# Causal attention rewritten: float32r stacks of 48 rows, two heads on the halves of the array, loads on GpSimd's queue

## The reference

```python
def _L0_attn_ref(x, Wq, Wk, Wv):          # x = layernorm of (8, 1024, 256), 16 heads of 16
    q = jnp.einsum('bte,hed->bhtd', x, Wq)
    k = jnp.einsum('bte,hed->bhtd', x, Wk)
    v = jnp.einsum('bte,hed->bhtd', x, Wv)
    scores = jnp.einsum('bhtd,bhsd->bhts', q, k)
    causal = jnp.tril(jnp.ones((T, T), dtype=bool))
    scores = jnp.where(causal, scores, -jnp.inf)
    scores = scores / jnp.sqrt(jnp.asarray(E, dtype=scores.dtype))
    w = jax.nn.softmax(scores, axis=-1)
    out = jnp.einsum('bhts,bhsd->bhtd', w, v)
    return jnp.transpose(out, (0, 2, 1, 3)).reshape(B, T, -1)
```

## Time and profile before

| | |
|---|---|
| median of three runs | 5360.85 us (5360.44 to 5373.26) |
| the profiled execution | 5367.81 us, span 5366.0 us |
| busy in the span | PE 4533.1, DVE 3604.8, ACT 2700.2, POOL 1211.8 us |
| mean granted clock of the array | 0.929 |
| attention | the first 1641 us or so |

### The profile page before, as it was taken

The page is one execution under the profiler, slowest core; times in us unless marked ns, Lnnn a source line. Parts: engine busy times, 40 slices in busy tenths (PEclk is TensorE's granted clock), DMA queues, the critical chain, the costliest instruction groups (busy, mean ns, idle before and its releaser), DMA issues. The chain is left out here.

```text
span 5366.0 us, 74844 instructions
## 1 busy us (share of the span) xinstructions
PE 4533.1 (84%) x23444; PEld 2361.1 (44%) x23444; DVE 3604.8 (67%) x6564; ACT 2700.2 (50%) x3784; POOL 1211.8 (23%) x784
## 2 busy tenths in 40 slices
PE   4888888887885888888888888888878999999999
PEld 1444344443432455445544554555553444444443
DVE  6677676676754878887888788555555555655653
ACT  0444444444453443444344434222226888888888
POOL 1000000000001333333333333000003455455454
PEclk7899899998997899989989999999998999999999
DMA  5422423324221000000000000000016666666664
GB/s 116 58 52 41 70 38 54 56 38 73 38 26 46 1 0 0 0 0 0 0 0 0 0 0 0 12 1 0 0 16 153 158 147 155 153 146 158 153 144 112
DMA packets 158004, 297.05 MB, mean 55 GB/s; under 512 B 41488, under 2 KB 88976, under 8 KB 141200
## 3 DMA queue, kind: packets, MB, share of 16 engines
q1 hardware_dynamic: 149760, 285.18, 25.9%
q10 hardware_dynamic: 7920, 7.87, 0.5%
HBM read 237.67 MB, written 55.31 MB: 55 GB/s over the span
## 5 line engine op out<-in xcount | busy, mean ns | idle before, releaser
L1686 ACT ACTIVATE gelu_out<-hidden,b_col 128x1024 f32<-128x1024 f32 x1024 | 1085.7, 1112 | 170.3 <-PE hidden L1600 167.4
L473 ACT ACTIVATE probsT<-scoresT 128x512 f32<-128x512 f32 (+3 forms) x1536 | 662.3, 505 | 735.0 <-PE scoresT L416 720.8
L530 DVE TENSOR_REDUCE maxima<-front 128x1 f32<-128x512 f32 (+3 forms) x1280 | 732.0, 631 | 145.0 <-PE front L381 96.9
L1666 POOL TENSOR_TENSOR combined<-combined,gated 128x512 f32<-128x512 f32 x480 | 616.4, 1284 | 675.8 <-DVE gated L1784 675.8
L890 POOL TENSOR_TENSOR pair_sums<-sims 128x1024 f32<-128x1024 f32 x256 | 488.0, 1914 | 1140.1 <-DVE pair_exp L1004 775.9
L1784 DVE SCALAR_TENSOR_TENSOR gated<-expert_out,b_col,gates_spread 128x512 f32<-128x512 f32 x480 | 359.2, 748 | 453.9 <-PE expert_out L1610 248.2
L1600 PE MATMUL hidden<-slice_stack,w_stack 128*128 128x512 f32 x2048 | 626.3, 428 | 15.1 <-ACT gelu_out L1686 15.1
L378 PE MATMUL front<-k_stack,q_stack 96*128 96x512 bf16 (+3 forms) x1536 | 478.7, 351 | 173.8 <-DMA k_stack<-split_scratch 101.3
L1610 PE MATMUL expert_out<-gelu_out,w_sb 128*32 128x512 f32 x4096 | 547.0, 606 | 30.7 <-DVE gated L1784 25.6
L1600 PEld LDWEIGHTS hidden<-slice_stack,w_stack 128*128 128x128 f32 x2048 | 352.7, 189 | 369.7 <-ACT gelu_out L1686 279.1
L413 PE MATMUL scoresT<-q_stack,k_stack 99*128 99x512 bf16 (+3 forms) x1536 | 479.8, 347 | 29.5 <-issue 17.0
(11 more groups left out here) (188 smaller groups left out, 6341.8 us busy)
## 6 DMA issues: line engine op xcount, KB each, us to landing
gates_spread<-gate_scratch SPq DMA_DIRECT2D x512, 256.0 KB, 4.7
slice_stack<-slice_scratch SPq DMA_DIRECT2D x128, 256.0 KB, 7.7
split_scratch<-split_parts SPq DMA_DIRECT2D x64, 384.0 KB, 2.6
q_stack<-split_scratch SPq DMA_DIRECT2D x96, 256.0 KB, 8.4
k_stack<-split_scratch SPq DMA_DIRECT2D x96, 256.0 KB, 17.5
slice_scratch<-slice_parts SPq DMA_DIRECT2D x32, 512.0 KB, 6.2
x_tiles<-in_L_attn_x SPq DMA_DIRECT2D x8, 1024.0 KB, 11.9
out_x<-x_tiles ACTq DMA_DIRECT2D x15, 512.0 KB, 4.8
```

The costliest lines, as they stand in the source:

```text
L473: nc.scalar.activation(PT[:, x % NPT, q0:(c + 1) * BANK], ST[i % 3][:, q0 - c * BANK:BANK], ACT.Exp, scale=SCALE).then_inc(probs_ready, 1)
L530: nc.vector.tensor_reduce(M2[:, hs, qt, kc], bank[:, 0:heads * w].rearrange("p (h k) -> p h k", h=heads), AX.X, ALU.max).then_inc(front_fr ...
L1666: nc.gpsimd.tensor_tensor(CM[:, par, hc, :], CM[:, par, hc, :], Y[:, u % 2, :], ALU.add)\
L1686: nc.scalar.activation(GH[:, k % 4, :, :], HP[k % HPB][:, :, :], ACT.Gelu, bias=b1c[:, u % E:u % E + 1])\
```

## The change

- Two parts instead of three, in float32r (fp32 storage): the stacks have 3 x 16 = 48 rows, and two rows for the maximum.
- Two heads share a stack tile. Head e of a pair lies on partitions 64e and up, and its matmuls run at `tile_position=(64e, 0)`. The masks stay matmuls of the whole array, after both heads of a pair.
- Two heads share an exponential: PSUM has 2 x 2 banks for scores, and an activation covers both heads. Values times probabilities go by halves of the queries: a group is (g, c, kt), its sum covers 512 queries and takes one bank, and outputs are copied and turned four times a half batch.
- The stack loads are issued by GpSimd, and wait until the scores of the half batch before are all done. The stores stay with SP; each waits for its own parts (`front_free` of its projection).
- The loops are written out; the order of all units is one list (`ORDER`), interleaved by cost numbers.

```diff
-    PARTS_Q = (0, 0, 1, 1, 0, 2)
-    PARTS_K = (0, 1, 0, 1, 2, 0)
-    K6 = len(PARTS_Q) * HS
-    K9 = K6 + 3
+    PARTS_Q = (0, 0, 1)
+    PARTS_K = (0, 1, 0)
+    KR = len(PARTS_Q) * HS
+    KM = KR + 2
...
+        cost = {"x": 0.5, "p": 2.4, "w": 0.9, "t": 1.4}
+        fills = value_units(n + 1) + projections(n + 2) + maxima(n + 1)
...
+        QS = sb("q_stack", [P, 2, NPAIR, T], F32R)
+        KS = sb("k_stack", [P, 2, NPAIR, T], F32R)
+        PT = sb("probsT", [P, NPT, G, BANK])
+        PC = sb("split_parts", [P, 2, 2, BANK], F32R)
...
+        ST = [ctx.enter_context(nc.psum_tensor(f"scoresT{i}", [P, 2, BANK], F32)) for i in range(2)]
+        PV = ctx.enter_context(nc.psum_tensor("pv", [P, BANK], F32))
...
+        @block.gpsimd
+        def _(pool):
+            for n in range(NS):
...
                 for c in range(2):
-                    sp.wait_ge(parts_stored[c], 16 * 2 * (n + 1))
-                if used_before(n):
-                    sp.wait_ge(pv_done, stack_released(n))
+                    pool.wait_ge(parts_stored[c], 16 * 2 * (n + 1))
+                if n >= 2:
+                    pool.wait_ge(scores_ready, 2 * NG * (n - 1))
...
+                            pool.dma_start(stack[at:at + HS, hf, :, :].bitcast(F32), rows[e]).then_inc(stacks_in[hf], 16)
...
+                def product(a, e):
+                    qt, kc = parts[a]
+                    rows = slice(64 * e, 64 * e + KR)
+                    return nc.tensor.matmul(F[(k - 1 + e) % 3][:, a * w:(a + 1) * w], QS[rows, hf, q, qt * P:(qt + 1) * P],
+                                            KS[rows, hf, q, kc * BANK:kc * BANK + w], start=True, stop=not diag,
+                                            tile_position=(64 * e, 0))
...
+            def scores(i, pr):
...
+                wait(pe, probs_ready, 2 * i + pr - 1)
+                bank = ST[pr]
...
+                for e in range(2):
+                    rows = slice(64 * e, 64 * e + KM)
+                    mm = nc.tensor.matmul(bank[:, e, at:BANK], KS[rows, hf, q, kt * P:(kt + 1) * P],
+                                          QS[rows, hf, q, c * BANK + at:(c + 1) * BANK], start=True, stop=not diag,
+                                          tile_position=(64 * e, 0))
+                for e in range(2) if diag else ():
+                    mm = nc.tensor.matmul(bank[:, e, at:at + P], identb[:, :], maskk[:, :], start=False, stop=True)
+                mm.then_inc(scores_ready, 1)
```

More of the change, by code:

```diff
@@ L160, in causal_attention @@
[L160 to L187, removed]
@@ new lines, in step @@
+    def step(n):
+        cost = {"x": 0.5, "p": 2.4, "w": 0.9, "t": 1.4}
+        fills = value_units(n + 1) + projections(n + 2) + maxima(n + 1)
+        costs = [0.1 + len(MAXB[u[4]]) * width(*MAXB[u[4]][0]) / 960 if u[0] == "m" else cost[u[0]] for u in fills]
+        pieces = []
+        for i, (g, c, kt) in enumerate(GROUPS):
+            w = BANK - first_query(c, kt)
+            pieces += [(("s", NG * n + i, pr), 0.15 + 2 * w / 1000) for pr in range(2)]
+            if NG * n + i > 0:
+                g1, c1, kt1 = GROUPS[i - 1]
+                pieces.append((("v", NG * n + i - 1), 0.5 * (BANK - first_query(c1, kt1)) / BANK))
+        total, spent, at, done = sum(w for _, w in pieces), 0.0, 0, 0.0
+        out = []
+        for j, (piece, w) in enumerate(pieces):
+            out.append(piece)
+            spent += w
+            if piece[0] == "v" and GROUPS[piece[1] % NG][2] == 0 and piece[1] > 0:
+                out.append(("o", phase(piece[1]) - 1))
+            while j >= 2 and at < len(fills) and (done * total <= spent * sum(costs) or fills[at][5:] == (1,)):
+                out.append(fills[at])
+                done += costs[at]
+                at += 1
+        return out + fills[at:]
@@ L191, in causal_attention, with phase @@
+    def phase(i):
+        n, (g, c, _) = i // NG, GROUPS[i % NG]
+        return 4 * n + 2 * g + c
+    ORDER = projections(0) + value_units(0) + projections(1) + maxima(0)
+    for n in range(NS):
+        ORDER += step(n)
+    ORDER += [("v", NG * NS - 1), ("o", 4 * NS - 1)]
+    FRONT = [u for u in ORDER if u[0] in "xpwmto"]
+    KF = {u: k for k, u in enumerate(FRONT)}
     with ExitStack() as ctx:
@@ new lines, in score_rows @@
+            def score_rows(k, n, g, pr, i, e):
+                hf, q = n % 2, 2 * g + pr
+                w, parts = width(*MAXB[i][0]), MAXB[i]
+                diag = parts[0][1] == parts[0][0] // 4
+                def product(a, e):
[4 more added lines that the diff above has]
+                                            tile_position=(64 * e, 0))
+                if (g, pr, i, e) == (0, 0, 0, 0):
+                    pe.wait_ge(stacks_in[hf], 16 * 12 * (n // 2 + 1))
+                bank_free(k)
+                k += 1 - e
+                if len(parts) == 1:
+                    mm = product(0, e)
+                    if not diag:
+                        mm.then_inc(front_done, 1)
+                for a in range(len(parts)) if diag and e == 1 else ():
+                    if len(parts) > 1:
+                        product(a, 0)
+                        product(a, 1)
+                    for e in range(2):
+                        mm = nc.tensor.matmul(F[(k - 1 + e) % 3][:, (a + 1) * w - P:(a + 1) * w], identb[:, :], maskq[:, :],
+                                              start=False, stop=True)
+                        if a == len(parts) - 1:
+                            mm.then_inc(front_done, 1)
```

502 lines of the change are left out of this document (209 added, 293 removed).

## The result

The changed kernel takes 5806.1 us (median of 4 runs, 5762.9 to 5830.3) against 5361.0, a ratio of 1.082, 95% interval 1.075 to 1.089. I had forecast 5270, a gain. The profiled execution took 5830.3 us. The attention ends near 2105 us instead of 1641, 464 us later; what follows it is as long as before. So the whole loss lies in the attention's steps.

A forecast was written before the change was run, and what follows sets the result against it. Part B was taken as array-bound with VectorE behind, part A as held by store and k-stack waits. 11.2 less in A, 5.2 more in B, times 15, gave -90, the start -5: 5270 us against 5360.9, range 5200 to 5345.

The forecast's parts named there:

- Array: maxima 24, scores and values 0.79 x (24 + 21.2) = 35.7, outputs and turned maxima 2: 61.7: The array's work in the later part of an attention step, from steady maxima on, summed to 61.7 us.
- B: Rest of a step (attention of a half batch) from the steady maxima on: array-bound, 64.0 us, 5.2 more than before.
- rival 3: Attention steps: half-array work and mask gaps could leave the clock at 1.2 GHz, 140 us a step, about 6,000; chance 0.05.
- Blocks at full clock: Score and maxima blocks: 0.62 us masked, 0.27 unmasked, 48 us a step.
- rival 5: Score and maxima blocks: a pair's heads run after each other, 15 us more; chance 0.30 together with rival 1.
- rival 1: The 64 masked blocks: switching eats the gain, +8.5 us a step, 5490; chance 0.30 together with rival 5.
- The price of 0.24 us: Masked blocks: going into tiles and out costs 0.24 us in all, weight loads included, as measured for column tiles.
- Part A: Step from issue of the stack loads to the steady maxima: 25.5 us, 11.2 less than before.
- VectorE's stop goes: Part A: stores wait only for their own data, ending VectorE's waits for them, 98.1 us in 1000 before.
- The load: Part A: the 3 MB stack load takes 26 us and lands 25 us into the step.
- rival 2: Part B: masked blocks at 0.45 us or less put the array beside VectorE's 48 us, 5120; chance 0.17.
- rival 4: Part A: GpSimd issues the loads late, A stays 36 us, +4.5 a step, 5430; chance 0.06.

The follow-up runs named there:

- e9: The changed kernel with each mask matmul issued three times, which changes no result: 5669 us.
- the benches: Three runs of the kernel before with matmul patterns repeated without waits at its start, each warm and after idle array; masked float32r pair of 512 columns: 0.65 us warm.
- e8: The changed kernel with bf16 stacks and the masks cut into two pieces of 64 rows on the row halves: 5208.7 us, ratio 0.971 to the kernel before.
- e7: The changed kernel with bf16 stacks instead of float32r, row halves and whole-array masks kept: 5371 us.
- b1_bench: First of the benches: the kernel before with eleven matmul patterns at its start, each warm and after idle array; masked float32r pair of 512 columns: 0.65 us warm.
- e2: The kernel before with only its 12 stack loads of a half batch moved from SP's queue to GpSimd's: 5335.9 us, ratio 0.994.

## Why the prediction was wrong

**The step that failed** is "Array: maxima 24, scores and values 0.79 x (24 + 21.2) = 35.7, outputs and turned maxima 2: 61.7" and its B = 64.0, which take every price at full clock. B was 90.3 and 102.2 us at a clock of 0.66 and 0.58. That was rival 3, to which I gave 0.05. Its price was near: a step of 140 us, 126 measured; blocks 78 us, and by the timeline at half clock 64 x 0.90 + 32 x 0.59 = 76. Its evidence stood in the earlier trace rows: an array busy 18.1 of 20 us, at 0.59. The prediction gives no reason for the twentieth; its sum B has the steady part of before for a model, which ran at 0.97 and more with the array as busy. e9 and the benches show that busy time doesn't carry the clock over to other blocks. What the runs put in the step's place is the clock: with it at 0.98 the same B takes 66.2 us.

Point by point:
- *Blocks at full clock.* Right in sum: 0.48 us at 128 columns and 0.66 at 512 (e9, less 0.22 for its extra masks), so 0.57 at the mean width, taken 0.62; unmasked 0.34, taken 0.27. Together 64 x 0.57 + 32 x 0.34 = 47 us for 48. That the array gets more work a step, not less, held.
- *Heads beside each other* (rival 5 out): 0.23 us for a pair of 512.
- *Switching* (rival 1): its break-even was 0.10 us more a block; at full clock it doesn't come to that. The price of 0.24 us was taken from column tiles, and row halves have 0.21. (The rival's own sum slips: blocks of 66 us give B = 80, not 78.5.)
- *Part A*: 34.0 and 26.1, mean 30.1, forecast 25.5. "VectorE's stop goes" was half right: 44.8 us of 98.1 stay, since a store now meets the loads in the DMA engines instead of behind them on a queue: one issued at 797.75 us, amid loads, landed 15.0 us later. The load lands as forecast, 24.8 us into the step at 663.96 us for 25, and the first maxima don't wait for it.
- *VectorE*: 66.2 and 61.0 us a step (14.8 + 51.4, 6.8 + 54.2), mean 63.6, forecast 61. It never became the bound (rival 2); in e8 it nearly does, as rival 2 had it for cheap blocks.
- *GpSimd's issue* (rival 4): 2.9 us for six issues in each A, and the other six just before it; no harm.
- *The last step*: 50 us at 0.97, forecast 51.

Not settled: what tips the clock in the kernel, and what keeps it down. In the two B's it falls near 702, 750, 828 and 876 us, each time behind the narrow maxima (128 to 384 columns) with which a group begins; of these the benches make 128 and 256 suspect. The one at 876 has hardly a gap before it (columns as in the earlier trace rows):

```profile
868.00:876.00 8.00, 7.84 (x62) 3.89 (x60) 4.66 (x9) 2.96 (x5) 0.00 (x0) 1.00 0.01 2
876.00:883.00 7.00, 7.00 (x34) 2.65 (x34) 4.35 (x8) 3.10 (x4) 0.00 (x0) 0.52 0.00 0
```

But it falls in other places too, and e7 with bf16 falls behind the same maxima (near 615 and 711 us). There it is back after 7 us, where the changed kernel stays down for 24 us from 702 and for 38 from 828. Why the two B's of a pair differ (0.66, 0.58, in e9 0.98, 0.83) is open as well.

## What to carry to other kernels

Before you price array work, ask what clock it will get: a record of the old kernel with a busy array at half clock is a warning, and short float32r matmuls were, in the benches, most of what brought it. Two heads on row halves run beside each other only while the array stays on the halves; a whole-array matmul in each block costs 0.21 us back, so put the mask on the halves as well, and keep the stacks bf16 where the precision allows it. A cheap test for a clock-bound stretch is to add whole-array work: if the time falls, as here, it was the clock.

## What the hardware showed that I had not expected

- Tripling the masks made the kernel faster (5806 to 5669 us).
- A clock once at 0.50 stays there under blocks that keep 1.00 when they find it: 0.65 us a pair warm, 1.05 after idle time, for the 31.7 us of the pattern. With four column tiles behind every two pairs it rose within 5 us.
- Matmuls of 48 float32r rows and 512 columns, one after another on a single half, dropped the clock as well (b1_bench: 0.64, then 0.50); pairs side by side did not.
- At a loop's return next to 3 MB of loads VectorE stood up to 13 us (e2); unrolled, it did not.
